# A transformer block on eight cores: first projections among the weight loads, ternary loads on POOL's queue, two buffers for xqT, the last output by column half

## The reference

```
x = x + attention(layernorm(x), w_qkv, w_out)      # 16 x 2048 tokens, D = 1024
x = x + ffn(layernorm(x), W1, b1, W2, b2)          # D = 1024, H = 4096
```

## Time and profile before

| | us |
|---|---|
| three timed runs | 1594.09, 1595.89, 1624.59 (median 1595.89) |
| the profiled execution | 1599.56 |
| its span (core 5, the slowest) | 1597.7 |
| spans of the eight cores | 1582.0 to 1597.7 |
| PE busy | 1503.5 (94%) |
| DVE, ACT, POOL busy | 1071.5 (67%), 797.2 (50%), 248.2 (16%) |
| HBM read, written by the core | 120.29 MB, 33.55 MB |

### The profile page before, as it was taken

How to read it: one execution, slowest core, us unless ns; L and a number is a source line. 1 busy time by engine, 2 the same in 40 slices (tenths; PEclk the granted TensorE clock), 3 DMA queues, 4 the chain that set the end, 5 groups by cost and what they waited for, 6 DMA issues and landing times.

```text
span 1597.7 us, 33901 instructions; the slowest of 8 cores (1582.0 to 1597.7 us)
## 1 busy us (share of the span) xinstructions
PE 1503.5 (94%) x11732; PEld 839.8 (53%) x11732; DVE 1071.5 (67%) x2695; ACT 797.2 (50%) x1835; POOL 248.2 (16%) x199
## 2 busy tenths in 40 slices
PE   2689999999899999979999999999999999999997
PEld 2466666666676666634444444444444444444443
DVE  2467888888789888757666666656666666656652
ACT  3567877777677777743434233333334233333331
POOL 0000012222133332103001010101101010101000
PEclk9889999999999999989999999999999999999999
DMA  9869788677657766434243433425253433424232
GB/s 299 267 151 225 199 225 241 198 212 193 205 148 191 192 190 163 118 85 103 67 112 67 98 82 77 103 62 110 66 112 67 99 80 78 101 63 109 66 86 53
DMA packets 277081, 214.26 MB, mean 134 GB/s; under 512 B 239280, under 2 KB 239408, under 8 KB 276912
## 3 DMA queue, kind: packets, MB, share of 16 engines
q1 hardware_dynamic: 272304, 195.31, 49.5%
q0 software_dynamic: 4608, 16.78, 2.8%
HBM read 120.29 MB, written 33.55 MB: 96 GB/s over the span
## 4 chain that ended last, share of the span: by engine, by line
PE 75%; DVE 10%; DMA 5%; issue 5%; ACT 2%; SPq 2%; POOL 1%; DVEq 0%; ACTq 0%; POOLq 0%
PE f L204 30%; PE av L204 28%; PE sc L204 15%; DVE msc L457 3%; DMA xlnT<-xln 2%; SPq L190 2%; DMA attnT<-attn 2%; DMA wst<-wqkv 1%; ACT probs L220 1%; DVE xr L240 1%; DVE lnc L327 1%; DVE tern L227 1%; PE tB L209 1%; PE tA L209 1%; DVE PT L253 1%
## 5 line engine op out<-in xcount | busy, mean ns | idle before, releaser
L204 PE MATMUL av<-W2q,hqT 128*128 128x512 fp8e4 x2048 | 448.9, 380 | 3.4 <-DMA hqT<-hq 3.4
L220 ACT ACTIVATE hbuf<-hb 128x512 f32<-128x512 f32 x256 | 160.7, 629 | 468.7 <-DVE hb L237 468.5
L204 PEld LDWEIGHTS av<-W2q,hqT 128*128 128x128 bf16 x2048 | 201.0, 98 | 246.3 <-issue 6.2
L220 ACT ACTIVATE probs<-msc,cells 128x256 bf16<-128x256 f32 (+1 forms) x512 | 250.8, 491 | 89.4 <-DVE cells L457 89.1
L204 PE MATMUL f<-xlnT,wqkv_sb 128*128 128x128 bf16 x4096 | 259.0, 223 | 25.3 <-DMA xlnT<-xln 13.8
L204 PEld LDWEIGHTS f<-xlnT,wqkv_sb 128*128 128x128 bf16 x4096 | 241.0, 100 | 39.6 <-issue 39.1
L204 PE MATMUL f<-W1q,xlnT 128*128 128x512 fp8e4 x1040 | 235.6, 379 | 0.1
L204 PE MATMUL sc<-W1q,xlnT 128*128 128x512 fp8e4 x1008 | 229.5, 381 | 3.3 <-DMA xlnT<-xln 3.3
L457 DVE CUSTOM_DVE_ANT_0 msc<-sc,masks 128x256 f32<-128x256 f32 (+1 forms) x512 | 182.2, 411 | 49.7 <-PE sc L204 40.6
L220 ACT ACTIVATE hq<-hbuf,konst,fhc 128x1024 f16<-128x1024 f32 x128 | 148.4, 1229 | 92.3 <-DVE fhc L225 85.5
L204 PEld LDWEIGHTS f<-W1q,xlnT 128*128 128x128 bf16 x1040 | 101.3, 98 | 122.3 <-issue 0.7
(11 more groups left out here) (81 smaller groups left out, 1385.5 us busy)
## 6 DMA issues: line engine op xcount, KB each, us to landing
stg<-w1t SPq DMA_DIRECT2D x64, 512.0 KB, 7.2
stg<-w2t SPq DMA_DIRECT2D x64, 512.0 KB, 5.1
xr<-xc SPq DMA_DIRECT2D x32, 512.0 KB, 6.0
x1sp<-xr POOLq DMA_DIRECT2D x32, 512.0 KB, 6.2
xr<-x1sp SPq DMA_DIRECT2D x32, 512.0 KB, 4.4
y<-msc SPq DMA_DIRECT2D x32, 512.0 KB, 3.2
wst<-wqkv SPq DMA_DIRECT2D x24, 512.0 KB, 17.7
wst<-wout SPq DMA_DIRECT2D x8, 512.0 KB, 19.9
```

What stands on the lines that cost most here:

```text
L204: return op("pe", lambda e: e.matmul(out=out, lhsT=lhsT, rhs=rhs, start=start, stop=stop), waits, sig)
L220: return op("act", lambda e: e.activation(out=out, in_=in_, func=func, **kw), waits)
```

## The change

It does the following.

1. All 16 first weight pieces are loaded at once, x2 behind piece 23. Q and K of tiles 0 and 1 are projected between the casts of pieces 8 to 23, two casts before each evacuation. V of tile 0 is computed by `v_pe_first`, with a wait for one cast per pair of matmuls. V of tile 1 becomes the filling of step 0; steps 1 to 3 have none. Tile 2 is normalized in step 1 and transposed by PE in step 2. The casts of w_out stand in steps 1 to 4 in place of 0 and 1.
2. The ternary loads are issued by POOL. The first six come in step 5 in place of 2, the tasks start at step 7 and end at step 116, and a step's loads stand behind its `task_pool`.
3. xqT has two buffers (xlnT0 and xlnT1), so that `xt(t)` waits for W1 of tile t - 2. `xt(1)`, `front_pool(2)`, `front_max(2)`, `front_q(2)` and `xt(2)` stand earlier. The last attention row is transposed by PE (`at_pe`).
4. `tq(t, r)` waits for quarter r of W2 of the tile before. W2 of the last tile runs one column half after the other, and its output is two instructions and two transfers of 256 KB.

```diff
--- before
+++ after
+        dma("sp", masks, masks_d, d_const, [tk["cb"]])
+        for i in range(8, 16):
+            piece_load(i)
...
             tk["xlnT", t] = tfree[b] = act(xlnT[t % 2], tb[b], AF.Copy,
-                                           [tok("X", t)])
+                                           [tok("X", t), tok("V", t - 2, 1)])
...
+        def v_pe_first(t):
+            w = [tok("xlnT", t), ffree[0], ffree[1]]
+            for c in range(DC):
+                for half in range(2):
+                    o = c * 3 * D + 2 * D + half * 512
+                    tk["V", t, half] = mm(
+                        fb[half], xlnT[t % 2][:, c * 128:(c + 1) * 128],
+                        wqkv[:, o:o + 512], c == 0, c == DC - 1,
+                        w + [tok("cast", 16 + c)], sig=(c == DC - 1))
+                    w = []
...
+        def at_pe(t):
+            b = tbank()
+            for c in range(DC):
+                tk["AT", t] = tr(tb[b][:, c * 128:(c + 1) * 128],
+                                 attn[:, c * 128:(c + 1) * 128], identb,
+                                 [tok("N", t, 0), tok("N", t, 1), tfree[b]]
+                                 if c == 0 else (), sig=(c == DC - 1))
+            tk["attnT", t] = tfree[b] = act(attnT, tb[b], AF.Copy,
+                                            [tok("AT", t), tok("O", t - 1, 1)])
...
-            task_ld[n] = dma("sp", stg[k], task_src(kind, i), d_stg[k],
+            task_ld[n] = dma("pool", stg[k], task_src(kind, i), d_stg[k],
...
         def xt(t):
-            tk["xqT", t] = dma_tr(xqT, xqb, d_xt,
-                                  [tok("xq", t), tok("W1", t - 1, 7),
-                                   tok("V", nt - 2, 1)])
+            w = tok("W1", t - 2, 7) if t >= 2 else tok("V", nt - 2 + t, 1)
+            tk["xqT", t] = dma_tr(xqT[t % 2], xqb, d_xt[t % 2],
+                                  [tok("xq", t), w])
...
         def tq(t, r):
...
-                                     [tok("hq", t, r), tok("W2", t - 1)])
+                                     [tok("hq", t, r), tok("W2", t - 1, r)])
...
-        def w2_pe(t, k0, k1):
+        def w2_pe(t, halves):
+            for k in range(32):
...
-                for n in range(2):
+                for n in halves:
                     p = mm(av[:, n * 512:(n + 1) * 512],
                            hqT[:, k * 128:(k + 1) * 128],
                            W2q[:, k * D + n * 512:k * D + (n + 1) * 512],
-                           k == 0, k == 31, w, sig=(k == 31 and n == 1))
+                           k == 0, k == 31, w,
+                           sig=(k % 8 == 7 and n == halves[-1]))
                     w = ()
...
+                if k % 8 == 7:
+                    tk["W2", t, k // 8] = p
+            for n in halves:
+                tk["W2n", t, n] = p
...
+        def out(t, half=None):
+            lo, hi = (0, D) if half is None else (half * 512, half * 512 + 512)
+            v = stt(yb[t % 2][:, lo:hi], av[:, lo:hi], fhc[t % 2][:, 7:8],
+                    x1r[t % 4][:, lo:hi], ALU.mult, ALU.add,
+                    [tok("W2n", t, hi // 512 - 1), tok("s2", t),
+                     tok("xbias", t), tok("y", t - 2), tok("EXP", nstep - 1)])
...
-        for i in range(12, 24):
+        for i in range(16, 24):
             piece_load(i)
-            if i == 15:
-                load_x(2)
-        load_x(3)
...
+        load_x(2)
+        nxt_cast = 8
+        for t, g in ((0, 0), (1, 0), (0, 1), (1, 1)):
+            for h in range(2):
+                qk_pe(t, g, h)
+            for h in range(2):
+                for i in range(nxt_cast, nxt_cast + 2):
+                    piece_cast(i)
+                    if i + 16 < npc:
+                        piece_load(i + 16)
+                nxt_cast += 2
+                qk_ev(t, g, h)
+            if (t, g) == (0, 1):
+                s_pe(0)
+                ttr(0)
+        load_x(3)
+        load_x(4)
         for hh in range(4):
             ex(0, hh)
+        v_pe_first(0)
+        for h in range(2):
+            v_ev(0, h)
...
-        for j in range(4, nstep):
+        for j in range(7, nstep):
             k = 1
-            if j < 40 and j % 3 == 0:
+            if j < 43 and j % 3 == 0:
                 k = 2
-            elif 40 <= j < 80 and j % 8 == 5:
+            elif 43 <= j < 80 and j % 6 == 5:
                 k = 2
...
+            if t == 0:
+                if c == 0:
+                    return (lambda: v_pe(1, h)), (lambda: v_ev(1, h))
+                return None, None
...
-            while j >= 2 and to_load and (prior[to_load[0]] is None or
-                               tok("task", prior[to_load[0]]) is not None):
-                task_load(to_load.pop(0))
             for n in at_step[j + 1] if nxt else ():
                 if tasks[n][0][0] == "q":
                     task_pool(n)
+            while j >= 5 and to_load and (prior[to_load[0]] is None or
+                               tok("task", prior[to_load[0]]) is not None):
+                task_load(to_load.pop(0))
...
+            if j == 2:
+                x_pe(2)
...
+            if j == 1:
+                ln1_nmr(2)
+                xln_(2)
...
-            if j < 2:
-                for i in range(24 + 4 * j, 28 + 4 * j):
+            if 1 <= j <= 4:
+                for i in range(22 + 2 * j, 24 + 2 * j):
                     piece_cast(i)
...
                 if c == 2:
                     for u in range(4):
                         gelu(0, u)
+                    front_pool(2)
                 if c == 3:
                     front_max(1)
                     front_q(1)
+                    xt(1)
...
-        at_tr(lt)
         for u in (6, 7):
             w1_pe(0, u)
             pre_gelu(0, u)
-        xt(1)
+        at_pe(lt)
...
         fh(0)
+        front_max(2)
+        front_q(2)
+        xt(2)
...
+            if it + 1 < nt:
+                w2_pe(it, (0, 1))
+            else:
+                w2_pe(it, (0,))
+                w2_pe(it, (1,))
+        for half in range(2):
+            out(nt - 1, half)
```

More of the change, by code:

```diff
@@ L136, in _build @@
     xq = xln.bitcast(F16)
-    xqT = xlnT[0]
+    xqT = xlnT
     yb = msc
@@ L171, in _build @@
         d_y = [sem("dY%d" % i) for i in range(2)]
-        d_xt = sem("dT")
+        d_xt = [sem("dT%d" % i) for i in range(2)]
         d_tq = [sem("dQ%d" % i) for i in range(4)]
@@ L839, in _build @@
         x_pe(0)
-        for i in range(8, 12):
-            piece_load(i)
-        dma("sp", masks, masks_d, d_const, [tk["cb"]])
-        tk["cm"] = (d_const, d_const.n)
-        for i in range(8):
+        for i in range(4):
             piece_cast(i)
@@ L953, in _build @@
                 ln2_sq(t - 2)
-            if c == 2 and t + 2 < nt:
+            if c == (2 if t else 1) and t + 2 < nt:
                 ln1_rstd(t + 2)
+            if j == 2:
+                x_pe(2)
             if f1 is not None:
                 f1()
-                e1() if c != 2 and not late else None
+                if c != 2 and not late:
+                    e1()
             for n in mine:
@@ L977, in _build @@
                 norm(t, 0)
[L978 removed]
+                if 1 <= t and t + 2 < nt:
                     ln1_nmr(t + 2)
@@ L1096, in _build @@
                 ln2_rstd(nt - 4, nt)
-            if it == 0:
-                front_max(2)
-                front_q(2)
-            if it + 2 < nt:
+            if it + 2 < nt and it >= 1:
                 xt(it + 2)
-                if it + 3 < nt:
-                    front_pool(it + 3)
-                    add_bias(it + 3)
-                    front_max(it + 3)
-                    front_q(it + 3)
-            w2_pe(it, 0, 32)
-        out(nt - 1)
-        QUEUE["sp"].append(([tok("y", nt - 2), tok("y", nt - 1)], None, None, 0))
+            if it + 3 < nt:
+                front_pool(it + 3)
+                add_bias(it + 3)
+                front_max(it + 3)
+                front_q(it + 3)
+            if it + 1 < nt:
[5 more added lines that the diff above has]
+            out(nt - 1, half)
+        QUEUE["sp"].append(([tok("y", nt - 2), tok("yh", nt - 1, 0),
+                             tok("yh", nt - 1, 1)], None, None, 0))
         def run(q):
```

55 lines of the change are left out of this document (19 added, 36 removed).

## The result

The changed kernel took 1615.18 us in the median of its runs against 1597.14 of the kernel before on the same chip: ratio 1.0104, 95% interval 1.0053 to 1.0154.

The account below looks back on a forecast made before the run. The MLP stage was taken as bound by its matmul count, so only PE's idle places could give time. Start 14.9, loads 3, passage 6.7 and end 6.0 sum to 30.6 us; off 1595.89 that gave 1565 us, range 1554 to 1579.

Parts of the forecast that it names:

- What bounds the kernel: Whole kernel: MLP stage bound by its number of matmuls, left alone; time can only come from places where PE idles.
- The start: Up to Q of tile 2: x2 later, projections between casts, tile 2 transposed by PE; 14.9 us less, bounds 12 to 17.
- thin steps: Start, tile 0's four steps, steps 1 to 3 without projection: 2.8 us each, 12.9 us for all four.
- The ternary loads: Attention stage: issuing 128 loads on POOL gains 6 us and costs 3, net 3 us, bounds -12 and +8.
- The gain of 6 us: Attention stage: fewer PE waits for transposes that stand alone on SP with the x loads; 6 us taken.
- Price of POOL on DVE: Attention stage: load issues on POOL stretch DVE instructions, costing 9 us of DVE and some 3 us of PE.
- Rival C: Attention stage: POOL becomes the new limit, through long issues and stretched DVE instructions; 1582 us, from 1575 to 1588, chance 0.24.
- The queues' fairness: DMA engines: the two kinds of queue are served in turn, which would favour the transposes; no size given.
- Rival D: Attention stage: POOL's queue makes `xln_` late in every tile, so xlnT misses its step; 1630 us, chance 0.03.
- The chances: Whole kernel against the one before: faster by over 2% 0.41, within 2% 0.56, slower by over 2% 0.03.
- The passage: Attention to MLP: earlier last output projection, no xqT wait for tile 2, less slow clock; 6.7 us less, bounds 4 and 10.
- The end: Last tile: no hqT wait, less slow clock, shorter last vector instruction and y landing; 6.0 us less, bounds 5 and 8.

Follow-up runs that it names:

- run 1: The changed kernel with its 128 ternary loads issued by SP again instead of POOL: 1572.71 us, ratio 0.9837 to the kernel before.
- e6_late_only: The kernel before with only the passage and end parts of the change; start, loads and tasks as before: 1585.25 us, ratio 0.9923.
- Run 7: The changed kernel with loads on SP and K's last two evacuations ahead of their casts: 1565.03 us, ratio 0.9797 to the kernel before.
- Run 8: Run 7 plus three bias loads behind tile 30's attnT transpose, and tile 30's W2 and output by column half: 1563.05 us, ratio 0.9780.
- run 4: Two versions of the changed kernel, ternary loads split between SP and POOL by step: moving 31 to POOL costs 32 to 38 us, the other 97 5 to 11.

## Why the prediction was wrong, point by point

**What bounds the kernel.** Right: the MLP stage is 801.2 us in both kernels, and only idle places changed.

**The start.** Forecast -14.9 us (bounds 12 to 17); -13.4 by the medians, 13.7 by runs 1 and 6. The reading that V would not overlap the casts held: it starts at 50.00, behind kT's evacuation (50.9 forecast), and ends at 55.30 (55.6). Q of tile 2 starts at 69.33 on core 3 (68.6); what was mis-sized are the thin steps, 14.0 us in place of 12.9, with one wait of 2.83 us for xln of tile 2 from POOL. Run 7 shows the cause of the missing overlap to be the one named.

**The ternary loads.** This is the term that failed: 3 us of gain, bounds -12 and +8, against a loss of 38.1 us (42.7 against run 1). It is the place that the prediction itself named: wrong above all if this stage moves by more than 8 us. The step that failed is the one that found nothing to pay on the side of the transposes: it priced a load on POOL only by what it does to POOL and DVE. Two sentences carried it. "On SP the transposes and the x loads now stand alone" was true of the queue and said nothing of the DMA engines behind it, which were 71% busy in the earlier trace rows. And "POOL waits no longer than `xln_` would have waited for its own DVE input" looked at what stands behind a load on POOL; it did not ask when the load itself goes out. With a load behind xln on xln's own engine, and the transpose on another engine behind the same xln, the load goes out 0.17 to 0.20 us ahead. The trace of before had a bound for that price, in the text's own first part: six loads on the same queue made xlnT land 12 us behind its issue. I used it as a thing that the change removes and not as the price of a load ahead. That the transpose of tile 3 "has two steps to land" failed by the same price, too. The burst of six goes out from 76.28 on; the transpose, issued at 86.58, has its last packet at 93.53, and PE waits (core 3):

```profile
95.30 3.52 PE L204 MATMUL f<-xlnT,wqkv_sb 128*128 128x128 bf16 x32 [4.95 <-DMA xlnT<-xln]
```

The gain of 6 us from transposes that stand alone can't be seen either. With the loads back on SP the stage takes 4.6 us less than before, but tiles 2 to 22 take the same (390.5 us, 389.6 before).

**Price of POOL on DVE.** I charged 3 us for stretched DVE instructions. There is none to be seen: the mean of the tern rows, which was 600 ns, is 472, and DVE is 7 us less busy:

```profile
L227 DVE TENSOR_SCALAR tern<-tern 128x1024 bf16<-128x1024 bf16 x64 | 30.2, 472 | 0.0
```

The reading that such an instruction is stretched when POOL runs was right: in the kernel before, the 34 that overlap POOL's arithmetic took 759 ns in the mean, the other 30 took 419. The loads' issues add nothing to it: in the changed kernel the 15 that overlap an issue on POOL and no arithmetic took 416 to 423 ns. Rival C, to which I gave 0.24, had 1582 us, from 1575 to 1588; the time measured lies 33 us above that, and its mechanism did not appear: where the load's issue is 0.53 to 0.78 us, POOL is no limit. The Trainium skill (SBUF — State Buffer, "SBUF: two separate sides") has loads issued by GpSimd starve while VectorE holds the shared ports; no row here shows it, in stretches where DVE was 87% busy: the loads landed 6.1 us behind their issue from either queue. The measurement decides.

**The queues' fairness.** I cited the Trainium skill (DMA: Bandwidth & Descriptors, "SWDGE vs HWDGE vs iDMA") for the two kinds of queue being served in turn, as favouring the transposes. The runs show the opposite effect: with a load 0.17 to 0.20 us ahead on the other queue the transpose's first packet comes 2.8 to 3.8 us behind its issue instead of 1.11, after 0.38 to 0.50 MB of other packets, nearly all of them from POOL's queue. That is about the load. Whether the engines don't alternate here, or the transpose is held before it reaches them, was not tried.

**Rival D** had the direction right, and its mechanism and its slack wrong. It made xlnT late by way of a late `xln_`. In the nine tiles concerned the transpose was issued 17.3 us behind the start of the tile's first group, where 15.7 is usual, and six of these tiles begin with such a wait themselves; from the issue on it took 5.1 to 7.4 us to land instead of 3.1. The slack was given as some 2 us and is 0.2 to 0.3 (1.7 once, 0.6 once in the nine). With its first packet 1.7 to 2.7 us later and a longer burst, PE waited 1.3 to 4.3 us. D counted one us lost for each us of delay; the nine waits are 28.4 us, and six groups at half clock add some 1.6 us each (an estimate from 3.57 and 1.96), 38 us in all. What D lacked is a reason for the delay, and the sentence "Nothing in the rows asks for it" should have been " asks for it".

**The chances.** I gave 0.56 to a time within 2% of the kernel before, and the time is there. That is luck: it came from a gain of 23 us and a loss of 38 us that the sum did not have.

**The passage.** Forecast -6.7; -6.0 between the stage borders, with O of tile 31 in addition earlier (1.26 us of wait instead of 4.76 on core 3). No wait for xqT of tile 2 is left. PE on core 3, against the earlier trace rows:

```profile
739.42 3.61 PE L204 MATMUL av<-wout_sb,attnT 128*128 128x512 bf16 x16 [1.26 <-ACT attnT L220]
...
770.49 3.62 PE L204 MATMUL sc<-W1q,xlnT 128*128 128x512 fp8e4 x16
```

The 31.07 us between these two starts were 36.09 before. Whether O runs at full clock varies from core to core of one execution: 3.61 us on cores 3 and 6 of the changed kernel, 5.1 to 5.3 on five others.

**The end.** Forecast -6.0 (bounds 5 to 8); measured -3.8. The wait for hqT went, and the low clock with it, as said. What was missed is late next (PE and DVE, against the earlier trace rows):

```profile
1601.17 13.97 PE L204 MATMUL av<-W2q,hqT 128*128 128x512 fp8e4 x64 [1.72 <-DVE msc L237]
...
1599.63 1.28 DVE L237 SCALAR_TENSOR_TENSOR msc<-av,fhc,xr 128x1024 f32<-128x1024 f32 x1 [4.51 <-PE av L204]
```

W2 of tile 31 writes the bank that `out(30)` reads. The 3.40 us for hqT had covered these 1.72. Run 8 took them out, and the end took 1.9 us less. The landing of the last y was under-sized the other way: 2.0 us behind its issue instead of 2.6, 0.6 less where I took 0.3. (The 0.6 that stands beside it in the prediction comes from a fit for transfers that GpSimd issues, and this one goes by SP; only the size agrees.)

**The sum.** With the forecast's 3 us for the loads and the other terms as measured, 1595.89 - 13.4 - 3 - 6.0 - 3.8 is 1569.7; run 1, which has everything but the loads on POOL, took 1572.71. So with that one word changed the time would have been inside the forecast range.

## What to carry to other kernels

Moving a transfer to another queue moves it against every transfer that is released by the same instruction: list, for each DMA on the critical path, what the new queue can put out within some microseconds ahead of it, and price that by what the trace shows for a transfer behind others. Measure the slack as well, from the issue of the transfer to the instruction that reads it, less the time to landing. One queue that holds both also keeps their order for nothing. A hold by semaphore on an in-order queue bunches what follows; look where the bunch lands before calling it a cure.

## What the hardware showed that I had not expected

- A DMA transpose (128x1024 bf16, SBUF to SBUF) with nothing under way has its first packet 1.10 to 1.18 us behind the issue and its last some 1.4 to 1.5 us later. In the changed kernel, with one 512 KB load 0.17 to 0.20 us ahead on the other queue, the first came 2.8 to 3.8 us behind the issue and the burst took 1.8 to 2.8 us.
- Over the 128 transposes of the table's five kernels (both kinds, up to 745 us) with another transfer issued within 4 us ahead, the delay of the first packet is about 1.0 us and 2.35 us for each MB that other transfers start to move in between (correlation 0.85). This describes the records and names no mechanism: a longer delay leaves room for more bytes, whatever causes it.
- The same 31 loads out of 128 carry three quarters or more of a 43 us loss. Where such a load does harm, its head start is 0.17 to 0.20 us.
- The last nine tile intervals of the attention stage took 174 us in the kernel before and in `e6_late_only`, and 168 to 170 in the changed kernel and in runs 1, 4, 7 and 8. So the gain comes with the new start or the new places of the tasks, on whichever queue the loads are; which of these moves gives it was not tried.
